# Sums of a graph layer: the two units of a strip in one PSUM bank, high and low halves in the same columns

## The reference

```
h   = relu(concat(x[src], edge_attr) @ W1.T + b1);  m = h @ W2.T + b2
agg = segment_sum(m, dst)
gi, gh = agg @ Wih.T + bih, x @ Whh.T + bhh          # GRU gates r, z, n
x1  = layernorm(x + (1 - z) * n + z * x)
s   = segment_sum(x1[dst], src);  deg = count of each src
out = layernorm(x1 + (s / max(deg, 1)) @ weight + x1 @ root_weight + bias)
```

## Time and profile before

| | us |
|---|---|
| median of three runs | 4579.04 (4568.23 to 4592.81) |
| profiled execution, own time | 4573.65 |
| its span | 4571.9 |
| PE busy | 3986.8 (87%) |
| PE weight loads busy | 3531.8 (77%) |
| DVE busy | 3296.7 (72%) |
| POOL busy | 3254.6 (71%) |
| ACT busy | 2362.2 (52%) |

### The profile page before, as it was taken

How to read it: one execution, slowest core, us unless ns; L and a number is a source line. 1 busy time by engine, 2 the same in 40 slices (tenths; PEclk the granted TensorE clock), 3 DMA queues, 4 the chain that set the end, 5 groups by cost and what they waited for, 6 DMA issues and landing times.

```text
span 4571.9 us, 90420 instructions
## 1 busy us (share of the span) xinstructions
PE 3986.8 (87%) x30332; PEld 3531.8 (77%) x30332; DVE 3296.7 (72%) x9964; ACT 2362.2 (52%) x4278; POOL 3254.6 (71%) x3198
## 2 busy tenths in 40 slices
PE   6477999888989898988898898989898999989875
PEld 6376788787879787877788787879787888878764
DVE  4454778686868686877778776868687777878655
ACT  2155555555555555555555555555555555555533
POOL 1677777777777777777777777777777777777700
PEclk8577898998989898999899998989898989989889
DMA  7454879696969697977879796969697887969655
GB/s 217 86 166 149 231 221 252 193 268 192 268 175 288 184 265 203 249 219 221 231 222 254 208 267 177 287 176 278 194 256 214 237 239 212 260 197 267 179 166 171
DMA packets 1017768, 998.76 MB, mean 218 GB/s; under 512 B 204167, under 2 KB 857548, under 8 KB 1016921
## 3 DMA queue, kind: packets, MB, share of 16 engines
q1 hardware_dynamic: 830878, 459.88, 39.3%
q10 hardware_dynamic: 84075, 321.56, 20.9%
q0 software_dynamic: 102352, 211.43, 17.5%
HBM read 655.22 MB, written 337.22 MB: 217 GB/s over the span
## 4 chain that ended last, share of the span: by engine, by line
PE 34%; POOL 29%; issue 15%; DVE 8%; DMA 7%; ACT 2%; SPq 0%; DVEq 0%; POOLq 0%; ACTq 0%
POOL ring L834 23%; PE stream_pse L1204 7%; PE stream_psw L1228 7%; PE stream_psa L1213 6%; PE stream_pse L1196 6%; POOL stream_yg L834 6%; PE stream_psw_third L1228 4%; DMA ring<-in_ea_blocks_dram 3%; DMA ring<-y,ring 3%; DVE stream_col L974 2%; PE stream_psw L1264 1%; ACT stream_a_sb L889 1%; DMA stream_yg<-y,ring 1%; ACT stream_hid L851 1%; DVE stream_xb L1021 1%
## 5 line engine op out<-in xcount | busy, mean ns | idle before, releaser
L834 POOL DMA_INDIRECT ring<-y,ring x2480 | 2541.2, 1025 | 759.5 <-issue 728.1
L889 ACT CAST stream_a_sb<-stream_psa 98x512 f16<-98x512 f32 x3125 | 1767.5, 585 | 1535.0 <-PE stream_psa L1213 1452.7
L1213 PE MATMUL stream_psa<-stream_col,stream_row 128*98 128x256 f16 x6250 | 1174.2, 291 | 152.9 <-ACT stream_a_sb L889 118.3
L1204 PE MATMUL stream_pse<-w1b,ring 128*128 128x128 f32 x6250 | 1054.8, 304 | 104.8 <-DVE ring L952 34.3
L974 DVE TENSOR_TENSOR stream_col<-iota_lo,stream_twin 128x1536 f16<-128x1536 f16 x1250 | 1020.9, 817 | 0.0
L1204 PEld LDWEIGHTS stream_pse<-w1b,ring 128*128 128x128 f32 x6250 | 897.9, 211 | 158.8 <-issue 65.4
L952 DVE TENSOR_TENSOR ring<-stream_pse,ring 128x384 f32<-128x384 f32 x1000 | 486.9, 487 | 695.9 <-PE stream_pse L1204 416.8
L1213 PEld LDWEIGHTS stream_psa<-stream_col,stream_row 128*98 128x98 f16 x6250 | 768.3, 133 | 236.5 <-ACT stream_a_sb L889 121.4
L1228 PE MATMUL stream_psw<-stream_z,stream_strip 128*128 128x257 f16 x5850 | 848.4, 275 | 23.4 <-DVE stream_sums L988 22.8
L1196 PEld LDWEIGHTS stream_pse<-stream_seg,stream_hid 128*128 128x128 f32 x6250 | 809.9, 205 | 0.8
L1196 PE MATMUL stream_pse<-stream_seg,stream_hid 128*128 128x32 f32 x6250 | 808.1, 279 | 0.0
(11 more groups left out here) (206 smaller groups left out, 2395.9 us busy)
## 6 DMA issues: line engine op xcount, KB each, us to landing
A<-stream_a_sb ACTq DMA_DIRECT2D x625, 490.0 KB
stream_strip<-A SPq DMA_DIRECT2D x1862, 160.0 KB
ring<-in_ea_blocks_dram SPq DMA_DIRECT2D x625, 160.0 KB
ring<-y,ring POOLq DMA_INDIRECT x2500
stream_yg<-y,ring POOLq DMA_INDIRECT x625
stream_col<-A SPq DMA_DIRECT2D x84, 96.0 KB, 2.5
prologue_xt<-in_xT_dram SPq DMA_DIRECT2D x14, 448.0 KB, 4.6
y<-prologue_ysb SPq DMA_DIRECT2D x14, 448.0 KB, 3.1
```

Source lines behind the costliest of these rows:

```text
L834: nc.gpsimd.indirect_dma_start(out=yg[s.c % YR][:, t, :], out_offset=None, in_=h.y, in_offset=bass.IndirectOffsetOnAxis(ap=idx[s.c // (PH ...
L889: nc.scalar.copy(a_sb[s.c % AR][0:RW, j, :], psa[BANK[j]][0:RW, :]).then_inc(a_out, 1)
L1204: last = nc.tensor.matmul(pse[half][:, (t - lo) * D:(t - lo + 1) * D], ea[s.c % 2][:, t * P:(t + 1) * P], h.w1b[:], start=True, stop=True)
L1213: last = nc.tensor.matmul(psa[BANK[j]][0:RW, e * LOS:(e + 1) * LOS], row1[s.c % 2][:, 2 * j + e, :], col1[s.c % 2][:, 2 * j + e, :], start ...
```

## The change

High and low part of a unit are now added up in the same 128 columns. So a unit needs 129 columns, and the two units of a strip lie side by side in one bank. Each matmul of 257 columns becomes two, of 129 and of 128 columns, with the same stationary operand. One signal, strip_done, and one addition of 258 columns follow for each strip. Strips take three banks in turn, the gate tiles two banks, and the last strips four banks instead of two pairs. The r_ready wait moves from unit 1 to unit 0, and in the last loop from strip 1 to strip 3. `count` now waits for its strip's addition.

```diff
-        psw2, psw_third = m.ps("psw", 1024), m.ps("psw_third")
-        psw = [psw2[:, 0:512], psw2[:, 512:1024], psw_third[:]]
-        pair = [x[:].rearrange("p (e c) -> p e c", e=2) for x in (pse2, psw2)]
+        psw = [m.ps(f"psw{k}") for k in range(3)]
+        last_bank = [pse[0], pse[1], psw[1], psw[0]]
+        def gate_bank(ph, t):
+            return psw[2 - t] if ph.col else psw[t % 2]
...
 SP, a strip's load
-                            sp.wait_ge(unit_done, ph.n(TS, 2 * (c - RING) + 3))
+                            sp.wait_ge(strip_done, ph.n(C, c - RING + 1))
...
 DVE
-            def unit_first(ph, u):
-                dve.wait_ge(unit_done, ph.n(TS, u + 2))
-                V.tensor_tensor(sums[:, u, :], sums[:, u, :], psw[(u + 2) % 3][:, 0:P + 1], ALU.add).then_inc(unit_part, 1)
-            def unit_second(ph, u):
-                dve.wait_ge(unit_part, ph.n(TS, u + 1))
-                V.tensor_tensor(sums[:, u, 0:P], sums[:, u, 0:P], psw[(u + 2) % 3][:, P + 1:XC], ALU.add).then_inc(unit_added, 1)
+            def add_strip(ph, c):
+                dve.wait_ge(strip_done, ph.n(C, c + 1))
+                V.tensor_tensor(sums[:, 2 * c:2 * c + 2, :], sums[:, 2 * c:2 * c + 2, :],
+                                psw[c % 3][:, 0:2 * (P + 1)].rearrange("p (e f) -> p e f", e=2), ALU.add).then_inc(strip_added, 1)
...
 DVE, body: done = {n: u // 2 for n, u in enumerate(units) if u % 2}; add_at(n) adds the strip that unit n of the step ends
-                adds(1)      # then rows(nxt)
-                adds(2)      # then cols(nxt, 0), add_gathered, add_segment
-                adds(3)      # then cols(nxt, 1)
-                adds(99)
+                add_at(0)
+                add_at(1)
+                add_at(2)
+                add_at(3, 4)
...
 DVE, last loop: add_high and add_low become
+            def add_last(c):
+                dve.wait_ge(strip_done, ITER * C + c + 1)
+                V.tensor_tensor(sums[:, 2 * c:2 * c + 2, :], sums[:, 2 * c:2 * c + 2, :],
+                                last_bank[c % 4][:, 0:2 * (P + 1)].rearrange("p (e f) -> p e f", e=2), ALU.add).then_inc(strip_added, 1)
             def count(c):
+                dve.wait_ge(strip_added, ITER * C + c + 1)
...
 PE
+            def accumulate(bank, e, tiles):
+                for n, (a, b) in enumerate(tiles):
+                    nc.tensor.matmul(bank[:, e * (P + 1):(e + 1) * (P + 1)], a, b[:, 0:P + 1], start=(n == 0), stop=False)
+                    last = nc.tensor.matmul(bank[:, e * (P + 1):e * (P + 1) + P], a, b[:, P + 1:XC], start=False,
+                                            stop=(n == len(tiles) - 1))
+                return last
             def unit(ph, u):
-                c = u // 2
+                c, e = u // 2, u % 2
                 if u == 0:
                     pe.wait_ge(z_ready, ph.n(1, 1))
-                if u == 1:
                     pe.wait_ge(r_ready, ph.n(1, 1))
...
-                if u >= 3:
-                    pe.wait_ge(unit_added, ph.n(TS, u - 1))
-                for t in range(PT):
-                    last = nc.tensor.matmul(psw[(u + 2) % 3][:, 0:XC], strip[c % RING][:, t, u % 2 * P:(u % 2 + 1) * P],
-                                            z[0][:, t, :], start=(t == 0), stop=(t == PT - 1))
-                last.then_inc(unit_done, 1)
+                    if c >= 3:
+                        pe.wait_ge(strip_added, ph.n(C, c - 2))
+                last = accumulate(psw[c % 3], e, [(strip[c % RING][:, t, e * P:(e + 1) * P], z[0][:, t, :]) for t in range(PT)])
+                if e:
+                    last.then_inc(strip_done, 1)
...
 PE, gate_work
-                    if t >= 3:
-                        pe.wait_ge(t_ready, ph.n(PT, t - 2))
+                    if t >= 2:
+                        pe.wait_ge(t_ready, ph.n(PT, t - 1))
...
 PE, after the stream
             pe.wait_ge(deg_in, LAST[1].n(16, 16))
+            pe.wait_ge(seg1_ready, BLOCKS)
             node_part(0)
...
 PE, last_unit
-                if c == 1:
+                if c == 3:
                     pe.wait_ge(r_ready, ITER + 2)
-                if c >= 2:
-                    pe.wait_ge(unit_added, ITER * TS + c)
+                if c >= 4:
+                    pe.wait_ge(strip_added, ITER * C + c - 3)
```

More of the change, by code:

```diff
@@ L1057, in body, with add_at @@
                 units = units_of(k) if k is not None and ph.p < ITER else []
-                ops = [(f, u) for u in units for f in (unit_first, unit_second)]
-                order = []
-                for n, u in enumerate(units):
-                    order.append((unit_first, u))
-                    if n:
-                        order.append((unit_second, units[n - 1]))
-                if units:
-                    order.append((unit_second, units[-1]))
-                def adds(n):
-                    for _ in range(n):
-                        if order:
-                            f, u = order.pop(0)
-                            f(ph, u)
+                done = {n: u // 2 for n, u in enumerate(units) if u % 2}
+                def add_at(*slots):
+                    for n in slots:
+                        if n in done:
+                            add_strip(ph, done[n])
                 if k == 0:
@@ L1312, in _ @@
             for t in range(3):
-                nc.tensor.matmul(psw[(t + 2) % 3][:, 0:3 * D], acc[:, PN + t * P:PN + (t + 1) * P], h.wc[:], start=False,
+                nc.tensor.matmul(gate_bank(LAST[1], t)[:, 0:3 * D], acc[:, PN + t * P:PN + (t + 1) * P], h.wc[:], start=False,
                                  stop=True).then_inc(g_done, 1)
@@ L1321, in last_unit @@
                     pe.wait_ge(z_ready, ITER + 2)
[L1322 removed]
+                if c == 3:
                     pe.wait_ge(r_ready, ITER + 2)
[L1324 to L1325 removed]
+                if c >= 4:
+                    pe.wait_ge(strip_added, ITER * C + c - 3)
                 for e in range(2):
[L1327 to L1331 removed]
+                    last = accumulate(last_bank[c % 4], e,
+                                      [(strip[c % RING][:, t, e * P:(e + 1) * P], z[0][:, t, :]) for t in range(PT)]
+                                      + [(late[c % RING][:, t, e * P:(e + 1) * P], z[1][:, t, :]) for t in range(3)])
+                last.then_inc(strip_done, 1)
             def turn_sums(c):
[L1334 removed]
+                pe.wait_ge(strip_added, ITER * C + c + 1)
                 reach(pe, mt_ready, c - 1)
```

45 lines of the change are left out of this document (14 added, 31 removed).

## The result

| | before | after |
|---|---|---|
| median of the runs, us | 4573.64 (4 runs, 4564.43 to 4592.81) | 4614.29 (4 runs, 4606.31 to 4616.17) |
| profiled execution, us | 4573.65 | 4616.17 |
| its span, us | 4571.9 | 4614.5 |
| first gather starts, us | 202.5 | 201.2 |
| last gather starts, us | 4334.1 | 4369.4 |

The ratio is 1.008, with a 95% interval of 1.0044 to 1.0117: 0.8% slower. The forecast was no measurable change, 4577 us; what came is the number of rival C, 4613.

A forecast was written before the change was run, and what follows sets the result against it. POOL's unbroken gathers bound the kernel: 202.5 us before the first, 4131.6 in them, 237.8 after, -2 for the last strips, a span of 4570; allowing for the runs' median, 4577 us. Range, 8 in 10: 4538 to 4620.

The forecast's parts named there:

- rival C: Strip stages: DVE's comparisons shift against the gathers, 20 ns more a gather, +36 us, about 4613 us; chance 0.11.
- Bound: Whole kernel: POOL's unbroken gathers set the time, 4131.6 of 4571.9 us; TensorE a close second.
- Matmuls: Products on PE: split into 129 + 128 columns, the extra weight load hides, 112 ns a product as before.
- the room of 22 ns: Products on PE: up to 22 ns more a product (10.6 / 490) costs nothing; beyond it PE decides.
- The additions of DVE: Strips on DVE: four additions become one, about 410 us of DVE time go, none on the path; value 0.
- the hold: Gathers beside DVE's fp16 comparisons: one can be held up, 1.36 us against 0.94.
- the spread over like stages: Stages with the same work: 1002 ns a gather in one, 1066 in another, mean 1025.
- the 20 ns a gather: Strip stages: the assumed lengthening of each gather from a worse place of the comparisons, +36 us.
- Waits: PE's moved waits (additions, r_ready, gate banks, seg1_ready): cost nothing, without cover under 5 us.
- the waits for landings about as now: DVE's waits for gathered rows: a sign of being right, unchanged from 160.3 + 30.9 us.
- rival D: PE saves its 36 us of waits and this shortens the kernel, to about 4550 us; chance 0.04.
- The last strips: Last 49 strips: they run at SP's pace, 3.78 us each; only the ends show, -2 us, between 0 and -5.

The follow-up runs named there:

- e7: The kernel before, unchanged, repeated on another chip (15): 4591.39 us, ratio 0.9985.
- e8: The kernel after, unchanged, repeated on chip 15 beside the kernel before: 4623.90 us, ratio 1.0062.
- e17: The kernel after with a step's third possible addition moved behind the second comparison of the columns: 4610.41 us, ratio 1.0069.
- e15: The kernel before without three of five matmuls per unit's product and four of five per segment product (sums incomplete): 4645.24 us, ratio 1.0173.
- e16: e15 with three additions of VectorE moved behind the second comparison of the columns: 4565.58 us, ratio 0.9985.
- e9: The kernel before with the addition for unit 3 moved behind the second comparison of the columns: 5730.58 us against 5645.42 on chip 9.

## Why the prediction was wrong, step by step

- **Bound.** Right: POOL's gathers, unbroken, from 201.2 to 4369.4 us, before and after.
- **Matmuls.** Right in kind, 6 ns short in size: 118 ns a product instead of 112, inside the room of 22 ns that the prediction gave. 17640 of them are in the stream, as forecast. 56 ns of the earlier trace rows became 59. PE's room shrank all the same. The 81 ns a matmul of the Trainium skill (TensorE: Matmul & The Clock Gate, section Back-to-back issue gap) were again not seen.
- **The additions of DVE.** This is the step that failed. "882 x 0.47 = about 410 us of DVE time go" was right, 3296.7 - 2875.3 = 421 us. "None of it lies on the path [...] Value: 0" was not: the time that went lay between the comparisons, and its going moved them against the gathers, which are the path. The prediction had seen the hold and the spread over like stages, and named both as rival C at 4613 us. That this is the time that came is in part luck: the 20 ns a gather was chosen from that spread and not computed, and it was 24 (1049 - 1025) in the steps with strips. It gave C 0.11, for "over 18 phases the places average out". They don't: a held gather ends 0.82 us behind the comparison that held it, so each comparison sets the phase for the next, and in the 90 even steps from 12 to 20 the second comparison now holds a gather 85 times. What should have been asked is what runs 1.12 us behind the first comparison. The earlier trace rows already hold the first part: the comparison at 2461.26 ends at 2461.92, the held gather at 2461.37 + 1.36 = 2462.73, 0.81 behind, and 0.3 later the next one starts. The second part, the new distance, is harder. The three additions between the comparisons last 0.20 us each to the next start, which taken from 1.8 us would leave 1.2, just past that instant. In the timelines of step 12 their waits for PE go as well, 1.12 us in all, and the wait for the edge product grows from 0.29 to 0.49. A sum without VectorE's waits would have missed it.
- **Waits.** Right: none of the moved waits shows. But "the waits for landings about as now" was one of the signs of being right, and it failed: 522 us instead of 191. VectorE has less to do and the gathers end later, which fits this wait; the gathers don't wait for it. PE's waits for the additions went and brought nothing, as rival D's 0.04 had it.
- **The last strips.** -2 us was forecast, +7.3 seen in one pair and +1.4 in the other, so the size is not settled. From one load of r to the next it is 3.77 us in the median, as forecast. SP's issues there are the pace, and some are slow. Two rows of SP after, an ordinary one and a slow one:

```profile
4558.20 1.25 SPq L747 DMA_DIRECT2D stream_strip<-A  x2
4559.49 2.31 SPq L747 DMA_DIRECT2D stream_col<-A  x2
```

  Of the issues behind the gathers 9 take over 0.9 us before and 11 in e7, and 14 in each of after, e8 and e17. What they take above 0.63 us is 7.1 us before and 13.1 after, 9.0 and 9.8 in the repeat, which goes with the +7.3 and the +1.4. Each of before's and after's, and 9 of e7's 11, stands beside a packet of the queue of instructions that has grown with the matmuls. Its row after (packets, MB, share; 257 before):

```profile
q8 instruction: 331, 5.42, 0.5%
```

  e15 and e16, with 175 such packets, have 8. That the fetch slows the issue is only argued from this coincidence.

So of the 42.6 us of the profiled pair, 36.6 are longer gathers, and these are holds by VectorE: the gathers outside its operations with two operands in SBUF take 944 ns in both kernels. That the place of the comparisons alone can move the time by as much is shown by e15 and e16. That in the change it is the five even steps which start it rests on the counts by step and on the replay, not on an undone edit.

## What to carry to other kernels

Where an engine runs without a gap and its operations differ in length, first find what lengthens them and at which instant that is decided; then work out where a change puts that instant, even if the time it saves lies on an engine with time to spare. When a hold sets the next start, the places don't average out: they lock. And to undo a placement, first find the steps in which it does harm, and look at what the engine waits for at that point: a mean over unlike steps hides both.

## What the runs showed of the hardware that was not expected

- A gather that starts inside an operation of VectorE with two operands in SBUF, with more than 0.12 us of it left, ends 0.82 us behind the operation's end; the share that has run before it starts makes no difference. This is so for the 16-bit comparisons of 0.42 to 0.95 us and for 32-bit operations of 0.81 us. Additions of 0.28 to 0.56 us with one operand in PSUM, copies and other operations of one operand don't do it: gathers inside them and outside of all operations last 944 ns on average before and after, and 944 to 948 in all the runs.
- The same instructions take 4570 to 4592 us on three chips and 5640 to 5710 on four, with a median gather of 944 ns on both, and on the second kind VectorE starts additions up to 5.1 us (e9) behind the start of a product's last matmul.
